# A third bank for the up products, products three units behind, weights shaped three ahead, and VectorE's sums first, in the expert stage of a linear-attention and mixture-of-experts layer

## The reference, cut

```python
xn = layernorm(x)                                   # x: 16 x 512 x 256, fp32: T = 8192 rows
Q, K, V = elu(xn @ Wq.T + bq) + 1, elu(xn @ Wk.T + bk) + 1, xn @ Wv.T + bv
ctx = (Q @ (K^T V)) / (Q . (sum K + 1e-6))          # linear attention in each batch
attn = ctx @ Wo.T + bo
scores = sigmoid(xn @ gate.T)                       # 16 experts in 4 groups
# 2 of 4 groups, then 4 of 16 experts for each row; weights normed, times 2.5
moe = sum over the 4 experts e of a row: w_e * silu(xn @ up_e) @ down_e
shared = silu(xn @ shared_up) @ shared_down
out = x + attn + moe + shared
```

## Time and profile before

| | us |
|---|---|
| median of 3 runs | 957.1 |
| lowest and highest | 952.12 and 961.92 |
| the profiled execution, its own time | 957.9 |
| its span, first to last instruction | 956.2 |

### The profile page before, as it was taken

The page is one execution under the profiler, slowest core; times in us unless marked ns, Lnnn a source line. Parts: engine busy times, 40 slices in busy tenths (PEclk is TensorE's granted clock), DMA queues, the critical chain, the costliest instruction groups (busy, mean ns, idle before and its releaser), DMA issues.

```text
span 956.2 us, 19692 instructions
## 1 busy us (share of the span) xinstructions
PE 775.9 (81%) x5280; PEld 722.9 (76%) x5280; DVE 695.0 (73%) x2411; ACT 556.6 (58%) x1172; POOL 577.1 (60%) x581
## 2 busy tenths in 40 slices
PE   8999999999999999996377778776777767768771
PEld 7898999898898988886367767676767667767661
DVE  7988898888888898898365766655566555657562
ACT  6777777767677766662255555455555455546450
POOL 1167776666667776667364656555556655556554
PEclk9999999999999999999697887988789887897886
DMA  6334555455444443333397888888788888888692
GB/s 189 114 142 164 193 188 183 177 189 189 155 169 160 147 139 116 118 114 123 112 350 231 253 271 269 260 256 263 241 253 251 261 256 269 264 271 264 193 306 78
DMA packets 137564, 194.64 MB, mean 204 GB/s; under 512 B 16608, under 2 KB 113008, under 8 KB 137456
## 3 DMA queue, kind: packets, MB, share of 16 engines
q1 hardware_dynamic: 106640, 108.69, 38.7%
q0 software_dynamic: 28064, 81.93, 22.2%
q10 hardware_dynamic: 2752, 2.77, 1.0%
HBM read 104.19 MB, written 105.04 MB: 219 GB/s over the span
## 4 chain that ended last, share of the span: by engine, by line
PE 60%; issue 10%; DVE 10%; another core or an unknown queue 10%; ACT 4%; POOL 2%; DMA 1%; ACTq 1%; DVEq 0%; SPq 0%; POOLq 0%
PE bank_a L330 20%; PE bank_y L330 18%; PE bank_x L330 15%; PE bank_a L1625 5%; DVE xn L1139 2%; PE bank_a L1450 1%; DVE xt_l L1352 1%; DVE xn L1370 1%; ACT xt_h L776 1%; POOL rows_by_expert L554 1%; POOL rows_by_expert L646 1%; ACT k_l_p L788 1%; ACT hs_h L819 1%; ACT k_h L788 1%
## 5 line engine op out<-in xcount | busy, mean ns | idle before, releaser
L554 POOL DMA_INDIRECT rows_by_expert<-xn,slots_now x192 | 196.8, 1025 | 121.2 <-PE bank_a L330 56.4
L1352 DVE TENSOR_TENSOR xt_l<-bank_a,xt_h 128x512 fp32r<-128x512 f32 x143 | 98.5, 689 | 133.9 <-ACT xt_h L776 112.8
L643 POOL DMA_INDIRECT rows_by_expert<-xn,f_id x128 | 122.9, 960 | 89.4 <-remote 30.3
L330 PE MATMUL bank_y<-we,hs_h 128*128 x572 | 137.5, 334 | 34.4 <-DVE xn L1370 10.5
L814 ACT ACTIVATE hid<-bank_x 128x256 f32<-128x256 f32 x143 | 55.3, 387 | 138.1 <-PE bank_x L330 59.0
L330 PEld LDWEIGHTS bank_y<-we,hs_h 128*128 128x128 f32 x572 | 101.9, 218 | 44.7 <-issue 43.6
L776 ACT CAST xt_h<-bank_a 128x512 fp32r<-128x512 f32 x143 | 83.7, 586 | 84.6 <-remote 45.5
L330 PE MATMUL bank_x<-xt_h,k_l_p 128*128 128x256 f32 x284 | 74.6, 322 | 49.2 <-DVE xt_l L1352 19.7
L330 PE MATMUL bank_x<-xt_h,k_h 128*128 128x256 f32 x288 | 75.6, 322 | 42.8 <-ACT k_h L788 17.4
L560 POOL DMA_INDIRECT rows_by_expert<-xn,slots_now x64 | 79.9, 1248 | 30.7 <-issue 13.8
L330 PEld LDWEIGHTS bank_x<-xt_h,k_l_p 128*128 128x128 f32 x284 | 57.7, 224 | 52.1 <-DVE xt_l L1352 31.2
(11 more groups left out here) (311 smaller groups left out, 2459.5 us busy)
## 6 DMA issues: line engine op xcount, KB each, us to landing
xn<-rows_by_expert SPq DMA_DIRECT2D x132, 272.0 KB
x_in<-rows_by_expert SPq DMA_DIRECT2D x80, 272.0 KB
rows_by_expert<-spare SPq DMA_DIRECT2D x22, 544.0 KB
out_dram<-rows_by_expert SPq DMA_DIRECT2D x16, 512.0 KB
x_in<-in_L_attn_x_dram SPq DMA_DIRECT2D x15, 512.0 KB
k_f<-rows_by_expert SPq DMA_DIRECT2D x16, 272.0 KB
q_f<-rows_by_expert SPq DMA_DIRECT2D x16, 272.0 KB
spare<-rows_by_expert SPq DMA_DIRECT2D x16, 272.0 KB
```

Source lines behind the costliest of these rows:

```text
L330: last = nc.tensor.matmul(dst, a, b, start=start and k == 0, stop=stop and k == n - 1, skip_group_check=mixed)
L554: G.indirect_dma_start(out=half_rows[:, :], in_=xn[:, c % NB, s, 0:RW], in_offset=None, out_offset=bass.IndirectOffsetOnAxis(ap=slots_now[ ...
L643: G.indirect_dma_start(out=half_rows[:, :], in_=f_y[u % YB][:, tile], in_offset=None, out_offset=offset).then_inc(added[u % CLS], 16)
L1352: V.tensor_tensor(f_l[u % 4], A[u % AB][:, :].rearrange("p (c s t) -> p c s t", c=KD, s=2), f_h[u % 4].bitcast(F32), ALU.subtract).then_in ...
```

## The change

From unit `LATER` = 18 on, TensorE makes the down product three units behind its up product, ScalarE copies weights three units ahead, and VectorE's loop has the sum of unit u - 3 as the first thing of its iteration u. The up products rotate over three banks in place of two: `bank_x0`, `bank_x1`, and the fourth bank of `bank_a`, which the turned rows give up (they keep three, `AB` = 3). There are four buffers for the hidden values and for each of their parts (before: two, three and three). GpSimd's first scatter of a unit waits for that unit's own down product. ScalarE's late loads of sums are issued two iterations later.

```diff
         WB = 8
-        AB = 4
+        AB = 3
         FROM = 14
+        LATER = 18
...
-        f_hid = [reused(hid, (1, UR), i * UR)[:, 0] for i in range(2)]
-        f_hh = [reused(hs_h, (1, UR), i * UR)[:, 0] for i in range(3)]
-        f_hl = [reused(hs_l, (1, UR), i * UR)[:, 0] for i in range(3)]
+        f_up = [X[0][:, 0:UR], X[1][:, 0:UR], A[3][:, 0:UR]]
+        f_hid = [reused(hid, (1, UR), i * UR)[:, 0] for i in range(4)]
+        f_hh = [reused(hs_h, (1, UR), i * UR)[:, 0] for i in range(4)]
+        f_hl = [reused(hs_l, (1, UR), i * UR)[:, 0] for i in range(4)]
...
         def down_with(u):
-            if u < 3 or u == FROM:
+            if u < 3 or u in (FROM, LATER):
                 return ()
-            return (u - 1 if u < FROM else u - 2,)
+            return (u - 1 if u < FROM else u - 2 if u < LATER else u - 3,)
...
                         if tile == 0:
-                            pool.wait_ge(fd_done, min(u + 2, UNITS))
+                            pool.wait_ge(fd_done, min(u + (2 if u < LATER - 2 else 1), UNITS))
...
                 act.wait_ge(fu_done, u + 1)
-                wait(act, fh_lo, u - 1)
-                S_.activation(f_hid[u % 2], X[u % 2][:, 0:UR], ACT.Silu).then_inc(fs_done, 1)
+                wait(act, fh_lo, u - 3)
+                if u == 2:
+                    act.wait_ge(attn_ready, SUB * B)
+                S_.activation(f_hid[u % 4], f_up[u % 3], ACT.Silu).then_inc(fs_done, 1)
...
                 act.wait_ge(fs_done, u + 1)
-                wait(act, fd_done, u - 2)
-                S_.copy(f_hh[u % 3], f_hid[u % 2]).then_inc(fh_hi, 1)
+                wait(act, fd_done, u - 3)
+                S_.copy(f_hh[u % 4], f_hid[u % 4]).then_inc(fh_hi, 1)
...
-                if 1 < u and u + 2 < UNITS:
+                if 1 < u <= LATER:
                     stage(u + 2)
+                if LATER <= u < UNITS - 3:
+                    stage(u + 3)
...
-                if u >= SUMS_BY_ACT:
-                    load_last_sums(u)
+                if u >= SUMS_BY_ACT + 2:
+                    load_last_sums(u - 2)
+            for u in range(UNITS - 2, UNITS):
+                load_last_sums(u)
...
-            for u in range(UNITS + 2):
+            for u in range(UNITS + 3):
...
                 next_experts(experts, mybir.EngineType.DVE, u)
+                if u >= LATER:
+                    for v in down_with(u):
+                        sum_up(v)
...
-                if u >= 4:
+                if 4 <= u < LATER:
                     for v in down_with(u):
                         sum_up(v)
...
-            for u in range(UNITS + 2):
+            for u in range(UNITS + 3):
                 next_experts(experts, mybir.EngineType.PE, u)
                 if u < UNITS:
                     pe.wait_ge(fx_lo, u + 1)
                     pe.wait_ge(fw_ready, u + 1)
-                    wait(pe, fs_done, u - 1)
-                    split3(X[u % 2][:, 0:UR],
+                    wait(pe, fs_done, u - 2)
+                    split3(f_up[u % 3],
```

More of the change, by code:

```diff
@@ L1393, in hidden_rest @@
                 dve.wait_ge(fh_hi, u + 1)
-                V.tensor_tensor(f_hl[u % 3], f_hid[u % 2], f_hh[u % 3].bitcast(F32), ALU.subtract
+                V.tensor_tensor(f_hl[u % 4], f_hid[u % 4], f_hh[u % 4].bitcast(F32), ALU.subtract
                                 ).then_inc(fh_lo, 1)
@@ L1643, in unit_down @@
                     last = split3(f_dn[v % 2][tile],
-                                  [(f_hh[v % 3][:, cols], f_hl[v % 3][:, cols], moving[0], moving[1])])
+                                  [(f_hh[v % 4][:, cols], f_hl[v % 4][:, cols], moving[0], moving[1])])
                 last.then_inc(fd_done, 1)
-            for u in range(UNITS + 2):
+            for u in range(UNITS + 3):
                 next_experts(experts, mybir.EngineType.PE, u)
```

## The result

The changed kernel takes 972.99 us (median of 4 runs, 969.29 to 973.79), the kernel before 958.28 us in the same comparison (median of 4, 952.12 to 961.92). The ratio is 1.015, 95% interval 1.0111 to 1.0189: slower by 1.5%, or 14.7 us. The interval leaves out 1, and the prediction had taken 1% as what such a measurement can tell.

The account below looks back on a forecast made before the run. The expert stage (533 to 935 us) was bound by PE's waits for late weight copies; 20 x 2.0 = 40 us saved, two thirds taken because GpSimd lets 44 us through: 957.9 - 27 = 931 us, range 918 to 947.

Parts of the forecast that it names:

- Weights three ahead: ScalarE's weight copies: PE makes one more step in each of 20 long waits ahead of up products, 40 us saved.
- rival B: Expert stage: PE's step only moves its idle time, or crowded DMA queues lengthen stalls; 955 us, chance 0.21.
- The forecast's sum of GpSimd: Expert stage: scatters 312 us plus 20 stalls of 2.28 us make 358 of 402, letting 44 us through.
- GpSimd's wait: First scatter of a unit starts about 1 us later against PE; taken as 0, 26 us if cover is gone.
- the 27 us: Expert stage: total gain forecast, two thirds of 40 us, since GpSimd's bound of 44 us is near.
- Third bank: Up products: with four hidden buffers gives nothing alone, but carries about half of the 40 us.
- products three behind: PE's down products: waits for sums two units back should shrink; end of kernel costs 0 to 2.0 us, taken 0.
- VectorE's sums first: VectorE's loop: waits for down products neither cured nor lengthened; taken as 0, 20 us either way.
- Rival A: Expert stage: shorter waits keep PE's clock up and all of GpSimd's 44 us are used; 914 us, chance 0.16.
- Rival C: Later scatters delay SyncE's landing waits, so rows come too late for PE's turns; 984 or about 975 us, chance 0.13.
- The DMA bound: Transfers, 533 to 935 us: floor 334 us by the profile's share, 241 us by the page; neither taken as tightest.
- G: Theory from the experiments, not the prediction: back-to-back GpSimd scatters hold PE's signals until some 1.3 us after the row.

Follow-up runs that it names:

- control: Changed kernel with one more register operation ahead of SyncE's and ScalarE's waits on table values; 961.56 us, 1.012, and 961.14 us, 1.0153 on chip 8.
- loose form: Kernel before, GpSimd's first scatter of unit u waiting from unit 16 on for the down product of u, not u+1; 941.43 us, 0.9917.
- the gaps: An unread power operation on GpSimd ahead of every second unit from 16 on, added to three kernels; on chips of the 950 us kind 0.9922, 0.9896 and 0.9886.
- the cut loads: Changed kernel loading from unit 24 on only 128 of each unit's 256 rows, output not the reference's; 964.08 us, 1.0168 on chip 8.
- near version: Kernel before, from unit 16 on first scatter awaiting its own down product, second the up product of u+3, not u+4; 981.69 us, 1.0318.
- the version with the power: Changed kernel with an unread power operation on GpSimd ahead of every second unit from 16 on; 940.99 us, 0.9922.

## Why the prediction was wrong, point by point

**Weights three ahead, 40 us.** PE's half of it came true beyond the forecast: the waits ahead of up products fell from 88.9 to 3.5 us, not to 50. But they were not on the path that sets the pace: PE's idle time only changed its place (109.5 us before, 103.4 after), as rival B had said of PE's step. Where GpSimd's rhythm is alike, the change is worth nothing (0.9916 and 0.9945 against 0.9917). On the chips of the 950 us kind two units take four scatters and the time until signals come through, 6.16 us, whatever PE does meanwhile. The forecast's sum of GpSimd, 312 + 46 = 358 us, had the right engine as the next bound and its stalls far too rare: 20 of 2.28 us, the number taken from ScalarE's long waits. GpSimd's own rows before the change, 533 to 935 us, say otherwise:

```profile
POOL rows_by_expert L643 <- remote: 55.4, 30, 2.3
...
POOL rows_by_expert L643 <- PE bank_y L330: 40.4, 22, 2.1
```

In all it stood idle for 1 us or more 56 times, 105.6 us. Less the 0.30 us of issue in each, that is 88.8, and 312.5 + 88.8 = 401.3 us fill the window of 402: there was no slack of 44 us to let through unless these stalls became shorter. In the better versions there are some 60 stalls of 1.2 us, in the changed kernel some 40 of 2.6 us, and both are there after every row, not only where ScalarE's long waits are. (A slip beside it: the first of the 20 long waits of PE is at 533.10, not at 548.18.)

**The step that failed** is the one on GpSimd's wait. The bound above explains why the 27 us did not come; this step explains why the kernel became slower. It dealt with the first scatter, whose wait the diff shows, priced it as about 1 us later against PE, and took 0. It did not ask where the second scatter's wait lands when products fall one step further behind. That wait, unchanged in its text, moved one step nearer to the sum. Scatters came closer together rather than later, rows grew to six, and ScalarE's stalls grew from 3.0 to 4.6 us. With that one wait set a step later the control goes from 1.012 to 0.9916. The prediction had said that ScalarE's 3.98 us gaps "stay as long and as many as before, some 20"; of 3.5 us or more there were 20, and there are 38.

**The releaser "remote"** was read rightly ("what PE has finished is told to the others late"), and then taken as fixed: "The change doesn't remove this." It isn't fixed; its length follows the kernel's own scatters, and the earlier trace rows had it: GpSimd's last scatter ends at 623.31 + 0.96 = 624.27, and ScalarE starts at 625.68, 1.41 us later.

**Third bank, products three behind.** The third bank was to carry half of the 40 us and products three behind to cost nothing. Nothing came of the first that could be measured. The second may not be free: with late sums and the later second wait, third bank, copies and products together are 0.8% slower than the kernel before in its loose form, 0.9998 against 0.9917. None of them was run alone.

**VectorE's sums first** at 0 with 20 us either way. The prediction compared with the kernel before, whose order is the same; no run shows that term alone. What was measured, 5 to 11 us against late sums with products three behind, is another comparison.

**Rival A**, more comes through with a higher clock, did not come: the granted clock of the window is 0.85 before and after.

**Rival C's mechanism**, SyncE's late loads, did not come: its landing waits fell from 24.7 to 13.1 us. Its sign, PE waiting ahead of turns, did: 9 waits for loaded rows, 7.8 us, beside the 49 inside a turn. The version with the later second wait has 30 such waits, 32.6 us, and is the faster, so they don't explain the loss. The direction of C was right and its reason wrong. **Rival B** held "stalls become longer" through crowded queues; the stalls did become longer, and with a seventh of the traffic gone (222 in place of 259 GB/s) they stayed so. What I lacked was a rival in which GpSimd's scatters are the cause and not the victim.

**The DMA bound** was put at 334 us by the share, and at 241 us from the Trainium skill (Perfetto Trace Analysis, Engine Utilization), an estimate from its ceiling of some 430 GB/s, with no run that told them apart. Chip 12 has 325 GB/s at a share of 0.97, so full share would be about 335 GB/s there, an estimate; the row before gives 258 / 0.83 = 311. No run came near the page's figure. On the chips of the 950 us kind neither bound decides, since cutting the share to 0.73 changed nothing.

**Open.** Which piece of the chip holds the signals was not found, nor why two chips do it and a third doesn't. That the rows of scatters set the time is shown by the edits of the second wait, in both kernels, and by the gaps; that the total of bytes does not is shown by the gaps and the cut loads. That the delay lies on PE's side, and not in how the others react, is argued: ScalarE and VectorE start within 0.13 us of one another at 586.64 and 586.77, and PE itself stands still between the transposes of one unit (585.90 and 586.65) just after the same row. The near version, with rows as long, has no such pause of PE, so the second point is weak. G as worded is too strict: of ScalarE's starts that came over 1 us after what they waited for, 35 of 59 in the near version fall inside a row, 6 of 41 in the changed kernel.

## What to carry to other kernels

When a loop's lag changes, list every wait that counts steps, on all queues, and ask how many steps away it now is; a wait that stands in no line of the diff can be the one that changes most. A wait on an engine that seems to be slack may be pacing it, so before loosening it look at what else starts when that engine pauses. And where several engines start together after "remote", look for the engine that had just stopped.

## What the runs showed of the hardware

- On two chips a long row of GpSimd's indirect DMAs, 1.27 us from start to start, delays what the other engines learn of TensorE's work, often until 1.3 us after the row (585.32 to 586.64; 0.84 us in the version with the power). Some signals pass at once in the first three scatters (11 of 51 in the changed kernel), none of 9 in the fourth. Rows of four cost 1.2 us of gap for 6.16 us of cycle, rows of six 2.6 for 9.95. A gap filled with another operation of GpSimd, 1.04 us long, lets signals through too.
- Adding 64 powers of 1.04 us to GpSimd took one kernel from 1.012 to 0.992 on one of these chips, and another from 1.032 on the one to 0.990 on the other. The bytes of the loads don't matter for it (259 or 222 GB/s).
- In the changed kernel TensorE pauses between the four transposes of one unit, 49 times and 40.4 us, without a wait in the program there. In the kernel before and in its near version it never does.
- On a third chip the same programs show no such delay: 69 of 73 starts of ScalarE within 0.1 us of TensorE's end, against 20 of 84 for the same kernel on chip 8. The kernel before takes 829.7 us there against 949, and the later second wait with late sums runs at 325 GB/s and a granted clock of 0.97. This difference between chips, 14%, is larger than anything that the edits did.
